# A two-layer graph kernel: first-layer source indices loaded once and copied into their slots by VectorE, and edge counts in four matmuls of 128 columns

## What is computed

```python
h = relu(layernorm(x))
ef = (relu(edge_attr @ We1 + be1) @ We2 + be2) * sigmoid(edge_weight * Wt + bt)
msg = relu(concat(h[src], ef) @ Wn1 + bn1) @ Wn2 + bn2      # one row per edge
x = x + segment_sum(msg, dst) + h
h = relu(layernorm(x))
x = x + relu(relu((h + segment_sum(h[src], dst)) @ W1 + b1) @ W2 + b2)
```

## Time and profile before

| | us |
|---|---|
| median of 3 runs (3261.2 to 3267.5) | 3265.5 |
| the profiled execution | 3264.75 |
| its span, first to last instruction | 3262.9 |
| POOL busy in the span | 2180.5 (67%) |
| PE busy | 2507.4 (77%) |
| DVE busy | 1661.6 (51%) |
| ACT busy | 946.1 (29%) |
| first gather of the first layer | 70.52 |

### The profile page before, as it was taken

How to read it: one execution, slowest core, us unless ns; L and a number is a source line. 1 busy time by engine, 2 the same in 40 slices (tenths; PEclk the granted TensorE clock), 3 DMA queues, 4 the chain that set the end, 5 groups by cost and what they waited for, 6 DMA issues and landing times.

```text
span 3262.9 us, 55219 instructions
## 1 busy us (share of the span) xinstructions
PE 2507.4 (77%) x15482; PEld 1659.5 (51%) x15483; DVE 1661.6 (51%) x3557; ACT 946.1 (29%) x941; POOL 2180.5 (67%) x2231
## 2 busy tenths in 40 slices
PE   3777787778878787878787777627788888888888
PEld 2555555555555565555555655522444454444445
DVE  5533333333333333333333333388877778777783
ACT  3333333333333333233333333231222222222221
POOL 2677777777777777777777777427566766666662
PEclk8888888888888888888889888657999898998999
DMA  5344444444444444444444444312222222222222
GB/s 175 112 128 129 129 127 129 130 125 129 128 131 124 131 125 130 127 130 129 128 129 129 129 129 129 62 71 68 57 60 59 67 61 61 64 60 66 60 66 63
DMA packets 185156, 341.45 MB, mean 105 GB/s; under 512 B 83611, under 2 KB 95388, under 8 KB 184960
## 3 DMA queue, kind: packets, MB, share of 16 engines
q0 software_dynamic: 80896, 165.82, 19.8%
q1 hardware_dynamic: 104162, 174.71, 15.3%
HBM read 329.06 MB, written 11.26 MB: 104 GB/s over the span
## 4 chain that ended last, share of the span: by engine, by line
POOL 29%; PE 23%; issue 21%; DVE 14%; DVEq 8%; DMA 4%; ACT 0%; POOLq 0%; SPq 0%; ACTq 0%; PEldq 0%
POOL big L470 29%; DVE arena L1142 6%; PE ps L655 5%; PE ps L666 5%; PE ps L745 4%; DMA big<-table,idx 4%; PE ps L760 2%; PE ps L646 2%; DVEq L1127 2%; DVE arena L1139 2%; DVE big L958 2%; DVEq L943 2%; DVEq L1142 1%; DVEq L1139 1%; PE ps L638 1%
## 5 line engine op out<-in xcount | busy, mean ns | idle before, releaser
L470 POOL DMA_INDIRECT big<-table,idx x2208 | 2157.1, 977 | 951.9 <-issue 671.5
L958 DVE TENSOR_TENSOR big<-ps,big 128x1024 f32<-128x1024 f32 x196 | 240.0, 1225 | 1250.5 <-DMA big<-table,idx 1247.1
L542 ACT ACTIVATE big<-big 128x1024 f32<-128x1024 f32 x196 | 207.2, 1057 | 1343.1 <-DVE big L958 1343.1
L745 PE MATMUL ps<-arena 128*128 128x500 bf16 x1416 | 416.1, 417 | 146.7 <-DVE arena L1142 145.6
L1142 DVE TENSOR_SCALAR arena<-iota_k,win_off,arena 128x500 bf16<-128x500 f16 x1416 | 500.3, 406 | 0.0
L666 PE MATMUL ps<-hot,big 128*128 128x64 f32 x3136 | 479.9, 307 | 7.6 <-DVE acc L951 7.6
L655 PE MATMUL ps<-wn1b,arena 128*128 128x128 f32 x1568 | 270.0, 343 | 258.3 <-DVE big L958 258.3
L666 PEld LDWEIGHTS ps<-hot,big 128*128 128x128 f32 x3136 | 461.0, 225 | 7.7 <-ACT big L542 7.7
L646 PE MATMUL ps<-arena,we 128*128 128x512 f32 x784 | 436.6, 684 | 3.9 <-ACT arena L532 3.9
L655 PEld LDWEIGHTS ps<-wn1b,arena 128*128 128x128 f32 x1568 | 249.1, 250 | 338.5 <-issue 333.5
L655 PE MATMUL ps<-wn1b,ef 128*128 128x128 f32 x1568 | 223.5, 301 | 172.1 <-DVE big L958 172.1
(11 more groups left out here) (140 smaller groups left out, 1918.5 us busy)
## 6 DMA issues: line engine op xcount, KB each, us to landing
arena<-in_ew SPq DMA_DIRECT2D x196, 512.0 KB
arena<-in_ea SPq DMA_DIRECT2D x196, 256.0 KB, 2.8
big<-table,idx POOLq DMA_INDIRECT x2208, 2.5
table<-big SPq DMA_DIRECT2D x7, 672.0 KB, 3.0
idx<-in_src SPq DMA_DIRECT2D x276, 4.0 KB, 1.6
xs<-in_x SPq DMA_DIRECT2D x7, 448.0 KB, 8.3
table<-nodes SPq DMA_DIRECT2D x7, 448.0 KB, 2.5
out<-xs SPq DMA_DIRECT2D x7, 448.0 KB, 2.5
```

Of the source, the lines that this page charges most:

```text
L470: pool.indirect_dma_start(to(u, q, t), None, table, bass.IndirectOffsetOnAxis(ap=idx[:, u, at:at + 1], axis=0))\
L745: m = pe.matmul(p_c[i % 2], hot_src[:, t, :], hot_key[:, t, :], start=False, stop=True, skip_group_check=True)
L958: dve.tensor_tensor(msg[:, u % 2, :, :, :].rearrange("p q t d -> p (q t d)"), p_pre2, rows[:, u, :, :, :].rearrange("p q t d -> p (q t d)" ...
```

## The change

All source indices, `src_tiles`, are loaded into `idx_all`, a part of `arena`, near the end of SP's parameter loads, with the first 32 columns again behind the last (`IDX`). VectorE copies eight columns into each of the four slots before its wait for `nodes_made`, and from then on `messages` copies those of the pair four later, after its wait for the gathers and ahead of its wait for `pre_mm`. The semaphores `idx_loaded` give way to `idx_made`, and `load_pair` loses its index load and the wait in front of it. In `aggregate` the counts of both blocks come after all sums, in four matmuls of 128 columns (two runs of 64) instead of eight of 64.

```diff
--- before.py
+++ after.py
@@ -129,7 +129,8 @@
         HOT = VT * (P + CK) // 2
         sizes = [EC, RING * BLK, RING * 2 * BLK, 2 * BLK]
 
-        arena = sb("arena", [P, max(sum(sizes) + 2 * BLK, 2 * (NTILE + VT) + NT * CROW + HOT)])
+        IDX = NTILE + RING * 2 * TB
+        arena = sb("arena", [P, max(sum(sizes) + 2 * BLK + IDX, 2 * (NTILE + VT) + NT * CROW + HOT)])
         assert NT * CROW <= ACC and 2 * NTILE <= NT * CROW
         cuts = [sum(sizes[:i]) for i in range(len(sizes) + 1)]
         tile_up, ea_s, tw, hid = (arena[:, a:b] for a, b in zip(cuts, cuts[1:]))
@@ -182,6 +183,9 @@
         efs = [ef, arena[:, sum(sizes):sum(sizes) + 2 * BLK].rearrange("p (q c) -> p q c", q=2)]
         assert RING % 2 == 0
 
+        at = sum(sizes) + 2 * BLK
+        idx_all = arena[:, at:at + IDX].bitcast(I32)
+
         half_at = RROW + 2 * TB * D - GT * D
         stages, stages2 = ([a[:, 0:GT * D].rearrange("p (t d) -> p t d", t=GT) for a in pair] for pair in (
             (big[:, RROW + 2 * TB * D:], big[:, half_at:]),
@@ -242,7 +246,8 @@
 
         ea_loaded = [sem(f"ea_loaded{u}") for u in range(RING)]
         ew_loaded = [sem(f"ew_loaded{u}") for u in range(RING)]
-        idx_loaded = [sem(f"idx_loaded{u}") for u in range(RING)]
+        all_idx_loaded = sem("all_idx_loaded")
+        idx_made = sem("idx_made")
         gathered = [[sem(f"gathered{u}{q}") for q in (0, 1)] for u in range(RING)]
         hid_mm = sem("hid_mm")
         ef_mm = sem("ef_mm")
@@ -344,6 +349,9 @@
                 sp.dma_start(to[:, :], b.rearrange("(a d) -> a d", a=1).to_broadcast([P, D])).then_inc(params_loaded, 16)
 
 
+            sp.dma_start(idx_all[:, 0:NTILE], src_tiles).then_inc(all_idx_loaded, 16)
+            sp.dma_start(idx_all[:, NTILE:IDX], src_tiles[:, 0:IDX - NTILE]).then_inc(all_idx_loaded, 16)
+
             sp.wait_ge(base_made, 2)
             sp.dma_start(base_d.rearrange("(p j) -> p j", j=NBJ), least[:, :]).then_inc(base_stored, 16)
             sp.dma_start(great_d.rearrange("(p j) -> p j", j=NBJ), great[:, :]).then_inc(base_stored, 16)
@@ -377,11 +385,6 @@
             def load_pair(at, b, u, first):
 
                 pair = at * RING + u
-                if not first:
-                    for q in (0, 1):
-                        sp.wait_ge(gathered[u][q], b * (16 * TB))
-                sp.dma_start(idx[:, u, :], src[bass.ds(pair, 1), :, :].rearrange("a p t -> p (a t)"))\
-                  .then_inc(idx_loaded[u], 16)
                 if not first:
                     sp.wait_ge(hid_mm, b * (2 * RING) + (2 * u + 2 - 2 * RING))
                 sp.dma_start(ea_s[:, u, :], ea[bass.ds(pair, 1), :, :].rearrange("a p c -> p (a c)"))\
@@ -480,12 +483,12 @@
 
             pool.wait_ge(table0_stored, 16 * NG)
             for u in range(RING):
-                pool.wait_ge(idx_loaded[u], 16)
+                pool.wait_ge(idx_made, u + 1)
                 gather_pair(table0, to_rows, u, gathered)
             with pool.Fori(1, sweeps * NBODY) as b:
                 for u in range(RING):
                     pool.wait_ge(pre_made, b * (2 * RING) + (2 * u + 2 - 2 * RING))
-                    pool.wait_ge(idx_loaded[u], b * 16 + 16)
+                    pool.wait_ge(idx_made, b * RING + (u + 1))
                     pool.wait_ge(agg_mm, b * RING + (u - 1))
                     pool.sem_inc(pairs_begun, 1)
                     gather_pair(table0, to_rows, u, gathered)
@@ -665,9 +668,8 @@
                     for t in range(TB):
                         pe.matmul(p_agg[:, q, 0, :], msg[:, m, q, t, :], hot_f[:, m, q, t, :],
                                   start=(t == 0), stop=(t == TB - 1))
-                    for t in range(TB):
-                        i = pe.matmul(p_agg[0:1, q, 1, :], ones[:, :], hot[:, m, q, t, :],
-                                      start=(t == 0), stop=(t == TB - 1))
+                for t in range(TB):
+                    i = pe.matmul(p_agg[0:1, :, 1, :], ones[:, :], hot[:, m, :, t, :], start=(t == 0), stop=(t == TB - 1))
                 i.then_inc(agg_mm, 1)
 
             def pair_step(b, u, since):
@@ -901,6 +903,9 @@
             dve.wait_ge(sweeps_made, 1)
             sweeps, start, total, bodies = load_params(dve)
 
+            dve.wait_ge(all_idx_loaded, 32)
+            for u in range(RING):
+                dve.tensor_copy(idx[:, u, :], idx_all[:, u * (2 * TB):(u + 1) * (2 * TB)]).then_inc(idx_made, 1)
             dve.wait_ge(nodes_made, NG)
             chain(dve.tensor_copy(p_iota, iota_s[:, :]))
 
@@ -950,11 +955,15 @@
                     dve.wait_ge(acc_added, total + q)
                     dve.tensor_tensor(to, p_agg[:, q, :, :], to, ALU.add).then_inc(acc_added, 1)
 
+            def copy_indices(u, at):
+                dve.tensor_copy(idx[:, u, :], idx_all[:, bass.ds(at, 2 * TB)]).then_inc(idx_made, 1)
+
             def messages(n, s, b, u):
 
-                dve.wait_ge(pre_mm, n + 2)
                 for q in (0, 1):
                     dve.wait_ge(gathered[u][q], (s * NBODY + b) * (16 * TB) + 16 * TB)
+                copy_indices(u, (b + 1) * (RING * 2 * TB) + u * (2 * TB))
+                dve.wait_ge(pre_mm, n + 2)
                 dve.tensor_tensor(msg[:, u % 2, :, :, :].rearrange("p q t d -> p (q t d)"), p_pre2,
                                   rows[:, u, :, :, :].rearrange("p q t d -> p (q t d)"), ALU.add).then_inc(pre_made, 2)
                 at = b * (RING * 2 * TB) + 2 * u * TB
```

## The result

The changed kernel took 3274.5 us (median of 8 runs, 3272.6 to 3279.8) beside 3265.5 for the kernel before (8 runs, 3260.2 to 3267.5): ratio 1.0032, 95% interval 1.0021 to 1.0043. The medians lie 9 us apart. Its profiled execution took 3274.88 us, with a span of 3273.0, which is 10.1 above the span of before.

What follows compares the result with a forecast made beforehand. GpSimd's gathers were taken to set the first layer's pace, with lateness from its wait for the sums and counts at TensorE's low clock. 1.6 + 1.8 + 4.5 + 0.2 = +8.1 us on 3264.75 gave 3273, range 3267 to 3282.

Steps and rivals of the forecast that it cites:

- The term of the late pairs: First layer's low-clock pairs: net 0.15 us for each of 28 late pairs and a few more, +4.5 us.
- Early gather: GpSimd's first gather at about 54.3 instead of 70.5 us, priced at nothing because pair 4 waits for pair 2's sums.
- Gathers beside the loads: Start: early gathers delay the edge attributes by 2 us, an index issue less saves 0.4; net +1.6 us.
- the load on the prologue: Loading all indices delays the block ends' stores and reload by some 2.3 us, less 0.5 of cover: +1.8 us.
- the 0.5 of cover: Prologue: TensorE, busy with transposes until 30.61, was to hide some 0.5 us of the 2.3 us delay.
- The copy, 0.2 us a late pair: VectorE's index copy ahead of L958 delays the add by 0.2 us (range 0.05 to 0.35), exposed only at 1.2 GHz.
- 28 pairs, and a few: First layer: some 28 low-clock pairs late by 1.15 us, plus a few newly late by a little, were to pay.
- the signs I had named as proving me wrong: Gathers over 1.27 us apart, low-clock pairs moving by more than ten, or pair 4 starting before 122.
- The counts, 0.05 us saved: Four count matmuls for eight at 1.2 GHz: 0.48 us for 0.54, 0.05 taken as saved; hidden at 2.4 GHz.
- SP's loads at another time: Attribute and weight loads go out about two pairs earlier and fall on other gathers; priced at nothing.
- The copy and GpSimd: VectorE's copy stretching GpSimd's gathers: taken as zero; as a rival, 11 to 31 us on top, 3284 to 3304, chance 0.15.
- the stretched gather of the earlier trace: Gather of 105.87, stretched to 1.38 us by a 1.04 us VectorE operation; evidence for the copy holding GpSimd.

Runs made afterwards that it cites:

- the last two experiments: GpSimd's wait for the sums left out of the changed kernel (3200.0 us, 0.9804) and out of the kernel before (3199.7 us, 0.9811).
- all_three: Changed kernel with the copy after the add, the index load after the block ends' reload, first gather held for the first edge attributes: 3272.3 us, 1.0031.
- counts_only_c: Kernel before with only the counts merged into four matmuls of 128 columns: 3263.4 us, 1.0007; without the suffix, on a 3.9 ms chip, 3896.4 us, 0.9921.

## Why the prediction was right, step by step

The time (3273 for 3274.5) and the sign were right, and so was the place: what makes GpSimd late is its wait for the sums, and the last two experiments show it directly. That the sum came so close is in part luck. The terms before pair 4 were 3.4 and measured 5.85. The term of the late pairs was 4.5 for 4.0, but it is the difference of two larger things that I didn't foresee. And the layers I had at nothing moved by -2.9 and +3.5. By its terms:

**Early gather, nothing.** Right, for the reason given: gathers did not lead to pair 4. Where they do lead, without the wait, the early start is worth 12.8 us.

**Gathers beside the loads, +1.6, and the load on the prologue, +1.8.** Together +3.4, measured +5.85. L864 came 2.37 us later (2.3 foreseen), but the 0.5 of cover didn't show: the loads of tile ends went out 2.36 later. From the attributes' issue to the first edge product it grew by 2.2 (2 foreseen); all_three keeps 1.6 of it with no gather beside the loads, which fits SP's closer issues and not the gathers. A further 1.6 us arose between the first edge product (+4.2) and pair 4. The clock moves the steps on the way in both directions: the second hidden products took 2.00 us for 1.11 and pair 2's sums 2.46 for 1.76, but pair 0's sums 1.73 for 2.51. How the 1.6 divide was not tried. Pair 4 came at 130.9, just outside the 127 to 130 that I had named.

**The copy, 0.2 us a late pair.** Right in size in three slots (the add 0.17 to 0.29 us later), and fully late pairs stand at 1.26 for 1.08, back at 1.10 with the copy moved. In slot 2 it is 0.47, above my upper end of 0.35: a register step and its gap, which I had not counted. Wrong also in what was multiplied: "28 pairs, and a few". Late pairs went from 36 to 63, most late by 0.46 only, so this was one of the signs I had named as proving me wrong (more than ten pairs moved). The body came out at +4.0 where +4.5 was said, but that is no proof of the term: with the copy moved it is 1971.8 in one profile and 1966.9 in another, and neither median fell by 4.5. By the arithmetic of the experiments the later adds are worth some 21 us of lateness, and the low stretches, now shorter, took away about 15 of the 29 us that were there: two large terms in place of one small one. How many pairs are late goes with the granted clock's pattern, which is another in each profile. With one profile a version, whether it belongs to the version or to the execution isn't shown.

**The counts, 0.05 us saved.** Two groups at 1.2 GHz and at 2.4 GHz in the timeline after (each row is four matmuls; the next instruction starts when the engine is free):

```profile
273.40 0.67 PE L672 MATMUL ps<-hot,ones 128*1 128x128 f32 x4
273.87 2.78 PE L649 MATMUL ps<-arena,we 128*128 128x512 f32 x4
...
1058.38 0.43 PE L672 MATMUL ps<-hot,ones 128*1 128x128 f32 x4
1058.66 1.93 PE L649 MATMUL ps<-arena,we 128*128 128x512 f32 x4
```

0.47 us where 0.48 was foreseen, 0.28 at the full clock. These matmuls go nearly by column, and not by instruction. Worth nothing in the total, as counts_only_c shows.

**SP's loads at another time, nothing.** Nothing that stands out. At the end pair 192 is 6.1 us late, where pairs 192 and 194 were 1.0 and 4.0.

**The copy and GpSimd, nothing.** Right: 946 ns a gather, and 1.25 us apart. So the stretched gather of the earlier trace rows has no like here. The Trainium skill (SBUF — State Buffer, "SBUF: two separate sides") says that a VectorE fp32 copy within SBUF keeps GpSimd from writing descriptors while it runs. The trace doesn't show that for this copy, int32 and 0.17 us, in the 166 gathers that had one beside them.

**Not priced.** The second layer, "which the diff leaves alone", took 3.5 us more. Between the layers 2.9 us were gained. This is open.

## What stays open

The second layer took 1013.9, 1016.1 and 1019.5 us in the three profiles without the index part, and 1019.5 to 1026.8 in the five with it (means 1016.5 and 1023.3); on the 3.9 ms chips 1246 and 1260, against 1260 to 1273. The waits in it, counts_only_c (2185 to 3201 us) and after it the changed kernel (2191 to 3215 us):

```profile
PEld ps L744 <- DVE arena L1141: 280.6, 289, 2.5
...
PE ps L744 <- DVE arena L1141: 148.8, 228, 2.2
DVE arena L1138 <- PE ps L744: 88.0, 105, 4.7
```

```profile
PEld ps L747 <- DVE arena L1151: 285.3, 292, 2.3
...
PE ps L747 <- DVE arena L1151: 152.6, 224, 2.1
DVE arena L1148 <- PE ps L747: 98.8, 121, 4.7
```

TensorE and VectorE wait for each other a little longer, at the same instructions. The clock is a part of the difference between the means: this layer spent 161 to 180 us at 1.2 GHz in the profiles without the index part and 170 to 187 with it. It is not the whole, since before and after both spent 180 us there and still lie 3.5 us apart. The text of this layer is the same; what of the index part reaches it (where buffers lie, where the programs start, how the layer begins) was not tried. It may well be why all_three, with pair 4 at 128.2 and the body back at 1966.9, still has a median 10 us above the kernel before; its profiled run, the fastest of it, is not the run that would show it. So of the 9 us about 6 arise before pair 4, and how the rest divides between body and second layer isn't settled.

## What to carry to other kernels

Ask of a wait not only who ends it but whether it is needed: the term that decided here was one wait, not what stood in front of it, and taking it out was worth seven times what the whole change moved. A price per late step can be foreseen to about 0.1 us, if the sequencer's steps behind the last wait are counted for every slot of the unrolled body: here one slot of four cost twice the others. But the number of late steps can't be carried over from the profile before when a varying clock sets it. And an edit that is hidden or given back can show its worth when the wait behind it goes (12.8 us of early gathers), so measure such parts again after the bound has moved.

## What the runs showed of the hardware

Two chips ran the kernel before in 3923 and 3930 us, the others in 3260 to 3266. On the former GpSimd has an extra wait of some 2 us ahead of a pair, put down to "remote", in 138 of the pairs (348 us, counts_only; the kernel before has no profile there). There the index part alone made the kernel 0.4% faster and the merged counts 0.7 to 0.8%. On the other chips both together made it 0.3% slower, and the counts alone changed nothing: a small change should be judged on more than one chip.

A wait of VectorE that stands behind the one that ends last costs 0.07 us though its count is long reached, and 0.26 us where a register step for that count comes with it (0.12, 0.19 and 0.38 from landing to add).
